# One block for the five stages of a post-norm attention and mixture-of-experts layer

## What is computed

```python
q, k, v = split(x @ Wqkv)            # 16 heads of 16; rotary tables on q and k
attn    = softmax(q @ k.T / 4) @ v   # inside each sequence of 512
x       = layernorm(x + attn @ Wo)
normed  = x * rsqrt(mean(x**2) + 1e-8) * norm_weight
shared  = relu(normed @ sw1 + sb1) @ sw2 + sb2            # 256 -> 1024 -> 256
w, idx  = top2(sigmoid(normed @ router_w.T)), divided by their sum
routed  = sum over the 2 experts e of w_e * (relu(normed @ ew1[e] + eb1[e]) @ ew2[e] + eb2[e])
out     = layernorm(x + shared + routed)                  # 8 experts
```

## Time and profile before

| | us |
|---|---|
| median of 3 runs (lowest, highest) | 1376.45 (1374.98, 1380.32) |
| the profiled execution, its own time | 1369.96 |
| its span, first to last instruction | 1368.1 |
| attention ends (last DVE instruction) | 583 |
| norm_and_route | 586 to 662 |
| shared_and_dispatch | 662 to 799 |
| experts | 804 to 1279 |
| combine | 1286 to 1368 |

### The profile page before, as it was taken

One profiled execution on the slowest core, in us unless ns is written; L12 is line 12 of the kernel. 1 busy time (PEld: TensorE's weight loads), 2 busy tenths in 40 slices (PEclk: granted clock), 3 DMA queues, 4 the chain that ended last, 5 costly groups with the idle time before them and its releaser, 6 DMA issues. The chain is left out here.

```text
span 1368.1 us, 29579 instructions
## 1 busy us (share of the span) xinstructions
PE 1256.6 (92%) x9440; PEld 955.3 (70%) x9440; DVE 1064.5 (78%) x2100; ACT 983.6 (72%) x2010; POOL 598.0 (44%) x550
## 2 busy tenths in 40 slices
PE   3799999999999999869899959999999999999594
PEld 2444444444444444258899959999999999999594
DVE  4688887888788877459576639988988888889498
ACT  5499988999889899748744436666666666666385
POOL 7332322222222210026446725666666666666461
PEclk8799999999999999979899979999999999999897
DMA  9000101010000000352032245666777766665344
GB/s 373 18 17 2 33 2 34 2 33 18 4 18 2 17 2 17 109 170 63 5 113 85 91 142 197 241 228 230 239 242 242 239 228 227 232 230 171 120 143 135
DMA packets 116021, 161.25 MB, mean 118 GB/s; under 512 B 16400, under 2 KB 97552, under 8 KB 114768
## 3 DMA queue, kind: packets, MB, share of 16 engines
q1 hardware_dynamic: 109104, 141.24, 31.1%
q0 software_dynamic: 6816, 18.75, 3.7%
HBM read 122.05 MB, written 37.52 MB: 117 GB/s over the span
## 5 line engine op out<-in xcount | busy, mean ns | idle before, releaser
L495 DVE TENSOR_REDUCE att_mx<-att_psA 128x1 f32<-128x512 f32 x512 | 336.1, 685 | 84.2 <-PE att_psA L297 78.9
L412 ACT ACTIVATE att_prob<-att_psB 128x512 f32<-128x512 f32 x512 | 296.8, 601 | 35.2 <-PE att_psB L307 23.5
L1524 ACT ACTIVATE exp_psU<-exp_psU,ew_b 128x256 f32<-128x256 f32 x312 | 126.6, 444 | 149.9 <-PE exp_psU L1481 149.9
L307 PE MATMUL att_psB<-att_qk 128*128 128x512 bf16 x512 | 196.4, 385 | 12.9 <-DMA att_qk<-att_mrow 9.6
L297 PE MATMUL att_psA<-att_qk 96*128 96x512 bf16 x512 | 196.0, 385 | 2.3 <-DVE att_mx L495 2.3
L1479 PE MATMUL exp_psU<-exp_xh,exp_w1h 128*128 128x256 f32 x624 | 176.7, 283 | 3.1 <-DVE exp_w1l L1553 2.2
L1464 PE MATMUL exp_psD<-exp_w2h,exp_hh 128*128 128x256 f32 x624 | 178.3, 286 | 0.0
L1480 PE MATMUL exp_psU<-exp_xl,exp_w1h 128*128 128x256 f32 x624 | 177.6, 285 | 0.0
L1465 PE MATMUL exp_psD<-exp_w2l,exp_hh 128*128 128x256 f32 x624 | 176.3, 283 | 0.0
L1481 PE MATMUL exp_psU<-exp_xh,exp_w1l 128*128 128x256 f32 x624 | 175.1, 281 | 0.0
L1466 PE MATMUL exp_psD<-exp_w2h,exp_hl 128*128 128x256 f32 x624 | 174.2, 279 | 0.0
(11 more groups left out here) (190 smaller groups left out, 3323.9 us busy)
## 6 DMA issues: line engine op xcount, KB each, us to landing
ew_w<-ew SPq DMA_DIRECT2D x40, 1024.0 KB, 6.6
exp_w<-ew SPq DMA_DIRECT2D x38, 1024.0 KB, 7.1
exp_xs<-slots_x SPq DMA_DIRECT2D x39, 260.0 KB, 4.3
slots_x<-pre_acc SPq DMA_DIRECT2D x9, 1024.0 KB, 15.2
out_g<-rows_y SPq DMA_DIRECT2D x32, 256.0 KB, 3.4
ew_b<-eb SPq DMA_DIRECT2D x39, 128.0 KB, 5.8
att_xt<-xT SPq DMA_DIRECT2D x8, 512.0 KB, 3.7
attn_rows<-att_ob SPq DMA_DIRECT2D x8, 512.0 KB, 3.0
```

What stands on the lines that cost most here:

```text
L307: pe.matmul(psB[B_BANK[n % U]][:, :], r[:, 1, kt * P:(kt + 1) * P], r[:, 0, :], start=True, stop=True).then_inc(s_bmm, 1)
L412: act.activation(prob[:, n % PR, :], psB[B_BANK[n % U]][:, :], ACT.Exp, scale=SCALE).then_inc(s_exp, 1)
L495: dve.reduce_max(mx[:, g % 2, n % U:n % U + 1], psA[A_BANK[n % U]][:, :], AX_X).then_inc(s_max, 1)
```

## The change

The five blocks become one. `Program` holds the one block and `ended`, a list of semaphores with values that tell that the last stage's compute is done; each engine's list for a stage now begins with waits on these (`after_last`) and has no drain or barrier. Semaphores are all held to the end of the kernel. Buffers of a new stage still lie where those of older stages lay.

```diff
+class Program:
+    def __init__(self, nc, ctx):
+        self.block = ctx.enter_context(nc.Block())
+        self.ended = []
+    def after_last(self, eng):
+        for s, v in self.ended:
+            eng.wait_ge(s, v)
...
 # attention, SP, period 29
                     sp.wait_ge(s_const, 2)
+                    sp.wait_ge(s_xl, B)
+                    norm.load_constants(sp, x, Wo, norm_w, router_wT)
                     for b in range(B - 1):
                         ...
                         norm.load_attention(sp, attn_out, b)
...
             for k in range(2):
                 sp.wait_ge(s_ost[k], 16 * (B // 2))
+            norm.load_attention(sp, attn_out, B - 1)
...
 # attention, POOL, two more steps after the eight of the start
+                lambda: pool.memset(norm.eps[:, 0:1], 1e-5),
+                lambda: pool.memset(norm.eps[:, 1:2], 1e-8),
...
+        pr.ended = [(s_onrm, NG)]                               # end of attention
...
 class NormInputs:                         # its spare region is attention's xt buffer
+    def load_constants(self, sp, x, Wo, norm_w, router_wT):
+        x_blk = x.rearrange("(b t p) d -> b p t d", t=self.NT, p=P)
+        sp.dma_start(self.wo, Wo.rearrange("(c p) n -> p c n", p=P)).then_inc(self.s_wo, 16)
+        sp.dma_start(self.first_x, x_blk[0]).then_inc(self.s_xr[0], 16)
+        sp.dma_start(self.rw, router_wT.rearrange("(c p) e -> p c e", p=P)).then_inc(self.s_w, 16)
+        sp.dma_start(self.nw, norm_w.partition_broadcast(P)).then_inc(self.s_w, 16)
...
 # norm_and_route, SP
-            sp.dma_start(wo[:, :, :], Wo.rearrange("(c p) n -> p c n", p=P)).then_inc(s_wo, 16)
-            sp.dma_start(xr[:, 0], x_blk[0]).then_inc(s_xr[0], 16)
-            sp.dma_start(rw[:, :, :], router_wT.rearrange("(c p) e -> p c e", p=P)).then_inc(s_w, 16)
-            sp.dma_start(nw[:, :], norm_w.partition_broadcast(P)).then_inc(s_w, 16)
-            given.load_attention(sp, attn, NB - 1)
+            pr.after_last(sp)
             for b in range(NB):
...
+                if b == 2:
+                    lists.load(sp, tri, marks, homes)           # mk, home, trs of the dispatch
...
 # norm_and_route, POOL: identity and eps are those of attention
-            for k, step in enumerate(( ...memset, affine_select, memset, memset... )):
-                step().then_inc(s_id, 1)
-                pool.wait_ge(s_id, k + 1)
+            pr.after_last(pool)
             pool.wait_ge(s_w, 32)
             pool.wait_ge(s_sw, 64)
...
+        pr.ended = [(s_lcp, TILES), (s_swl, 2 * SWP)]           # end of norm_and_route
...
 # shared_and_dispatch
-            sp.dma_start(mk[:, :], marks).then_inc(s_k, 16)
-            sp.dma_start(home[:, :, :], ...).then_inc(s_home, 16)
-            sp.dma_start(trs[:, :], tri).then_inc(s_k, 16)
+            pr.after_last(sp)
+            weights.load_spare(sp, homes)
...
-            for k in range(2):                                  # POOL
-                pool.wait_ge(s_sc[k], 2 * per_sem)
+        pr.ended = [(shared.added, NB)]
+        return [(s, TILES * 16) for s in s_sc]                  # "sent"
...
 # experts, SP
-            sp.dma_start(spare[:, :, :], homes[...]...).then_inc(s_spare, 16)
+            pr.after_last(sp)
+            for landed in sent:
+                sp.wait_ge(*landed)
...
 # experts, POOL: no identity at the start, no wait at the end
-            pool.memset(ident[:, :], 0.0).then_inc(s_id, 1)
-            pool.affine_select(out=ident[:, :], ...).then_inc(s_id, 1)
+            pr.after_last(pool)
...
-            for k in range(2):
-                pool.wait_ge(s_st[k], 16 * RT * ((NL + 1 - k) // 2))
...
 # experts, ACT (DVE the same with rows_lo and w1_lo)
-            rows_hi(Tile(0))
+            pr.after_last(act)
             for q in range(WP):
                 w1_hi(Tile(0), q)
+            rows_hi(Tile(0))
...
+        pr.ended = [(s_y, NL)]
+        m.landed = [(s_st[k], 16 * RT * ((NL + 1 - k) // 2)) for k in range(2)]
...
 # combine, DVE and ACT
-            dve.memset(eps[:, :], 1e-5).then_inc(s_eps, 1)
+            pr.after_last(dve)
             shared.rows_lo(dve, Nth(0))
...
-            act.wait_ge(s_eps, 1)
...
 # combine, SP
+            pr.after_last(sp)
+            for landed in m.landed:
+                sp.wait_ge(*landed)
```

More of the change, by code:

```diff
@@ L78, in attention @@
         sin = a.sb("sin", [P, NT, DH], F32)
-        xt = a.sb("xt", [P, 2, DC, L], F32)
+        xt = norm.spare[:, :].rearrange("p (k c l) -> p k c l", k=2, c=DC)
         wh = a.sb("wh", [P, DC, 3 * D], F32R)
@@ L654, in norm_and_route @@
         psL = [a.ps(f"psL{i}", [P, 512], F32) for i in range(2)]
-        s_wo, s_w = a.sem("projection_weights"), a.sem("weights")
+        s_wo, s_w, s_xr = given.s_wo, given.s_w, given.s_xr
         s_sw = a.sem("shared_weights")
         s_swh, s_swl = a.sem("shared_hi"), a.sem("shared_lo")
-        s_xr = [a.sem(f"residual_loaded{i}") for i in range(2)]
-        s_id = a.sem("identity")
         s_ttr = a.sem("attn_turned")
@@ L852, in _, with __init__, load @@
                     dve.bn_aggr(mv[:, i % 4, :], st[:, i % 4, :]).then_inc(s_var, 1)
+        pr.ended = [(s_lcp, TILES), (s_swl, 2 * SWP)]
+class DispatchInputs:
+    def __init__(self, pr, ctx, marks, T, D):
+        a = Steps(pr, ctx, "sent")
+        self.trs = a.sb("trs", [P, P], F32)
+        self.mk = a.sb("mk", [P, marks.shape[1]], F32)
+        self.home = a.sb("home", [P, 2, T // P], F32)
+        self.rows = a.sb("rows", [P, T // P, D + HOME], F32)
+        self.s_k = a.sem("constants")
+        self.s_home = a.sem("homes_loaded")
+    def load(self, sp, tri, marks, homes):
+        sp.dma_start(self.mk[:, :], marks).then_inc(self.s_k, 16)
+        sp.dma_start(self.home[:, :, :], homes[:, SPARE // P:].rearrange("p (k t) -> p k t", k=2)).then_inc(self.s_home, 16)
+        sp.dma_start(self.trs[:, :], tri).then_inc(self.s_k, 16)
 class Nth:
@@ L984, in add, with shared_and_dispatch @@
         dve.tensor_tensor(acc, self.psD[n.parity][:, :, :], acc, ALU.add).then_inc(self.added, 1)
[L987 removed]
+def shared_and_dispatch(pr, homes, slots_x, lists, weights, m):
     TILES, E = m.logits.shape[1], m.logits.shape[2]
@@ L1265, in load_first, with experts @@
             load(sp, 0, e)
-def experts(nc, slots_x, weights, homes, rows_y, m):
+def experts(pr, slots_x, weights, sent, ident, rows_y, m):
     w1, w2, b1, b2 = weights.w1, weights.w2, weights.b1, weights.b2
@@ L1291, in experts @@
         xs = a.sb("xs", [P, 2, RT, slots_x.shape[1]], F32)
-        home = a.sb("home", [P, 4, RT], U32)
-        spare = a.sb("spare", [P, 2, RT], F32)
+        w1h = a.sb("w1h", [P, DC, HID], F32R)
+        w1l = a.sb("w1l", [P, DC, HID], F32R)
+        spare, s_spare = weights.spare, weights.s_spare
         xh = a.sb("xh", [P, 2, DC, LT], F32R)
@@ L1775, in layer @@
     with ExitStack() as ctx:
-        given = NormInputs(nc, ctx, T, P * rope_cos.shape[1], D)
-        attention(nc, xT, Wqkv, rope_cos, rope_sin, attn, slots_x, given)
-        m = Carried(nc, ctx, given.acc, T, D, E, sw1.shape[1], LT)
-        weights = ExpertWeights(nc, ctx, ew1, eb1c, ew2, eb2)
-        with nc.sbuf_tensor("all_rows", [P, T // P, D + HOME], F32) as rows:
-            norm_and_route(nc, x, attn, Wo, norm_w, router_wT, sw1, sb1c, sw2, sb2, rows, given, m)
-            shared_and_dispatch(nc, tri, marks, homes, slots_x, rows, weights, m)
-        experts(nc, slots_x, weights, homes, rows_y, m)
-        combine(nc, rows_y, out, m)
+        pr = Program(nc, ctx)
+        given = NormInputs(pr, ctx, T, P * rope_cos.shape[1], D, E)
+        attention(pr, x, xT, Wqkv, rope_cos, rope_sin, Wo, norm_w, router_wT, attn, slots_x, given)
+        m = Carried(pr, ctx, given.acc, T, D, E, sw1.shape[1], LT)
+        with ExitStack() as until_used:
+            weights = ExpertWeights(pr, until_used, ew1, eb1c, ew2, eb2, LT)
+            with ExitStack() as until_sent:
+                lists = DispatchInputs(pr, until_sent, marks, T, D)
+                norm_and_route(pr, x, attn, sw1, sb1c, sw2, sb2, tri, marks, homes, lists, given, m)
+                sent = shared_and_dispatch(pr, homes, slots_x, lists, weights, m)
+            experts(pr, slots_x, weights, sent, given.ident, rows_y, m)
+        combine(pr, rows_y, given.eps, out, m)
 def kernel(L0_attn_x, L0_attn_Wqkv, L0_attn_Wo, L0_ffn_norm_weight, L0_ffn_router_w, L0_ffn_sw1, L0_ffn_sb1,
```

135 lines of the change are left out of this document (68 added, 67 removed).

## The result

The median went from 1376.47 us (1374.98 to 1380.32) to 1356.01 us (1353.51 to 1356.50), four runs each: ratio 0.984, 95% interval 0.983 to 0.986. The forecast was 1360.0 us, range 1354 to 1367.

The account below looks back on a forecast made before the run. The prediction looked to the four unequal seams between stages, not their arithmetic. Its terms, 7.0 + 6.7 + 0.2 + 5.5 - 3.0 = 16.4 us, took the median from 1376.45 to 1360.0 us, eight in ten from 1354 to 1367.

Parts of the forecast that it names:

- the norm stage's rate changed: Norm stage: the forecast counted itself wrong if this stage's rate, rather than its start, had changed.
- attention ended later than 588: End of attention: 586 us was expected in place of 583; later than 588 would show the forecast wrong.
- (a): Experts to combine: SP waits for landings alone, so combine's loads go out earlier; gain 7.0 us, bounds 6.1 and 10.5.
- Rival 2: Both scatter seams: idle time is no drain but paid by others too; total gain 4.7 us, 1371.7 us; chance 0.08.
- (b): Shared to experts: list 0's load goes out earlier and weights are split before the rows; gain 6.7 us, bounds 5.7 and 7.3.
- (c): Norm to shared: the 0.28 us barrier goes and waits remain; gain 0.2 us, bounds 0 and 0.9.
- (d): Attention to norm: the last bias lands earlier, so POOL's first multiplication starts earlier; gain 5.5 us, bounds 3.5 and 6.5.
- Rival 3: Norm stage: ACT or DVE late, or bias issued late, so (d) gains only 3 us; 1362.5 us; chance 0.15.
- (e): End of attention: constants queued ahead of the last group's maxima make PE wait longer; loss 3.0 us, bounds 0 and 5.
- rival 1: Last group of attention: the maxima are not held up by the constants; gain 19.4 us, 1357.0 us; chance 0.22.
- Inside the stages the change alters no arithmetic: Whole kernel: the prediction's premise, so it looked for gains only in what lies between the stages, at four seams.

Follow-up runs that it names:

- set 2: Four kernels on one chip beside the kernel before (1372.97 us): the kernel before again, its reordered buffers, the changed kernel with barriers at quiet seams, and the changed kernel again.
- late_constants: Changed kernel with the four constants issued where they were before, behind the landing of attention's last sequence: 1395.18 us, ratio 0.991 to the kernel before.
- blocks_at_quiet_seams: Changed kernel with a new block (drain and barrier) put back at attention to norm and norm to shared: 1356.09 us, ratio 0.988 to the kernel before.
- before_new_order: Kernel before with only the experts' SBUF buffers allocated in the changed kernel's order: 1366.94 us, ratio 0.996 to the kernel before.
- before_again: The kernel before, unchanged, profiled once more on the chip of set 2: 1371.34 us.
- after_third: The changed kernel, unchanged, run again on the chip of set 2: 1353.65 us, ratio 0.987 to the kernel before.
- split_later: early_again, with POOL's first multiplication not waiting for the shared expert's weights and their splitting 6 tiles later: 1388.19 us, ratio 0.981 to the kernel before.
- sets 1 and 2: Two sets of follow-up runs, each on its own chip; the unchanged changed kernel was rerun in both: 1390.52 us (0.987) and 1353.65 us (0.987).
- early_again: Changed kernel with the four constants issued in period 25 in place of 29, repeated on another chip: 1395.65 us, ratio 0.986 to the kernel before.
- sets 1 and 3: Two sets of follow-up runs, each on its own chip, beside the kernel before at 1409.21 us and 1414.0 us.

## Why the prediction was right, and where its terms were off

The time fell inside the range and on the forecast's side. Two of the signs that the prediction had named against itself did appear: the norm stage's rate changed, beside its start, and attention ended later than 588 (at 594.54; with the start and the loop of the kernel before it would be 588.3). Both are taken up below. By its steps:

- **(a) Experts to combine, 7.0.** Measured 6.7 (11.45 to 4.70; also 6.7 in set 2). That it is the block's end and not a landing that others pay too is shown: a block put back there costs 5.26 us twice (2.45 to 7.71). Rival 2 fell. The other 1.5 us go with POOL's wait for the landing in front of that end (9.2 against 7.71). The early start of the other engines brought nothing: from the first load on the stage took 1.1 us longer (0.2 in set 2).
- **(b) Shared to experts, 6.7.** Last scatter to first product 15.04 to 8.05 us, 7.0. Of this 6.1 is the seam and 0.9 the earlier split of the weights. The prediction called the moved `spare` load off this path; it was on it, with 0.4 of the 6.1 us. Same mechanism as (a), but shown here only between whole kernels.
- **(c) Norm to shared, 0.2.** The last logits end at 669.47, ACT's first instruction of the next stage starts at 669.50, in place of 0.28 us behind the earlier trace rows.
- **(d) Attention to norm, 5.5.** Measured 6.2, in set 2 5.2; 15.3 us was forecast for the gate and 14.6 to 15.4 came. late_constants gives 5.6 us to the loads' place, blocks_at_quiet_seams some 0.4 to the barrier. Rival 3 fell.
- **(e) The maxima held up, 3.0.** This is the term that was mis-sized: 5.3 us (5.5 in set 2). The wait was seen almost right (4.80 us, "about 4" forecast), and rival 1 fell with it. What was missing is that PE comes out of such a pause at half clock: 3.8 us more wait and 1.5 us for the restart at 0.50. I had bounded it at 5, by the loads alone. The maxima, issued at 570.13, released PE only at 577.30, behind a burst that ended at about 575. (The rows that the prediction cites for the queue's order are of ten transfers, not nine.) The Trainium skill, page "DMA: Bandwidth & Descriptors", section "Queues, rings and completion order", says that a DMA engine takes the descriptors of one issuer's ring in ring order; the trace agrees in that the maxima did not get past the burst (4.1 to 5.2 us to landing in place of 1.7), while two of them landed before the last load that was issued ahead of them.

Together 6.7 + 7.0 + 0.3 + 6.2 - 5.3 = 14.9 us, 1.5 less than summed. The medians differ by 20.5. The other 5.5 us are sought in stretches where I took the change for nothing:

- The experts' pace, -5.7 us (470.53 to 463.85 less the 0.9 of (b)). "Inside the stages the change alters no arithmetic" was true and not enough: it moves buffers. before_new_order shows 26 of 42 products in 400 us from addresses alone.
- The norm stage's rate, +2.0 us in the first profile and +1.3 in set 2. Its last 12 us, before_again first, then after_third (granted clock is the third number from the end):

```profile
657.70:663.70 6.00, 4.37 (x31) 3.58 (x29) 5.39 (x25) 5.04 (x21) 2.87 (x5) 1.00 0.00 0
663.70:669.70 6.00, 4.07 (x25) 3.72 (x25) 0.84 (x2) 4.31 (x14) 0.29 (x1) 0.66 0.04 10
```

```profile
655.90:661.90 6.00, 4.36 (x29) 3.64 (x29) 5.58 (x25) 5.03 (x21) 2.87 (x5) 0.94 0.00 0
661.90:667.90 6.00, 5.41 (x28) 5.31 (x26) 0.16 (x1) 3.92 (x14) 0.54 (x1) 0.50 0.00 0
```

 With nearly as many products in the last 6 us (25 and 28), PE needs 5.41 us in place of 4.07: in the tail, where it is partly idle, the clock falls to half (1.2 GHz) some 2.5 us sooner, counted from POOL's first multiplication (both pairs of rows begin 48 us after it). Why sooner was not found; it does so with barriers at the quiet seams too (59.64 us). That is the 1.3 us of set 2. Of the 2.0 us of the first profile the greater part, 1.2 us, arises at the stage's start: POOL's seventh multiplication comes 12.80 us behind its first in place of 11.55 (603.82 to 615.37 before, 609.15 to 621.95 after), and the granted clock of these first 12 us is 0.72 in place of 0.81.
- The rest is scatter between executions: the loop differs by up to 7 us between executions of either kernel (503.8, 505.9 and 509.6 us in the three profiles of before and its variant, 506.5 to 511.0 in the eleven of after and its variants). It took 7.2 us more in the first profile after, and with as long a loop as before the two profiled executions would be 21 us apart. Whether the change has a small part in it is open: the three have a mean of 506.5, the eleven of 509.1, on different chips.

So the forecast was right for four of its five steps. That it came within 4 us is in part luck: a cost that was put too small (e) and a gain that it did not have (the pace) went against each other.

**A better version.** split_later has the lowest ratio of all, 0.981 (0.978 to 0.984), against 0.984 (0.983 to 0.986) for the changed kernel in the first comparison and 0.987 in sets 1 and 2. It was run on one chip only, and not beside the changed kernel; beside early_again it is 0.5% faster with intervals that overlap a little, and its landmarks (7.1 us) say the same.

## What to carry to other kernels

Look at what POOL had in flight when a block ends: behind arithmetic a barrier here costs some 0.3 to 0.4 us, right behind an indirect DMA 5 us and more, and a wait on the landing's semaphore replaces it. A load that is "moved to where there is time" goes into a queue: name what stands behind it, and move it past the last small transfer that PE waits for (here four periods earlier saved 5.5 us there and cost at most 0.7 at the gate). And before taking a gate at a seam as a queue's fault, ask whether the waiting instruction needs what it waits for: in split_later 7 us came from taking out one such wait, with the splits of the weights moved later to allow it.

## What the hardware showed that I had not expected

- SBUF addresses change the pace of a stage that PE bounds, without idle time and at full clock: 11.805 us a list against 11.716 by the order of the buffers alone. The changed kernel, whose buffers lie differently again and which has other differences too, takes 11.657.
- On two of the chips PE lost 30 to 50 us in the shared stage while the indirect scatters ran. Stretches of 25 us, after_third (set 2) and then early_again (set 3):

```profile
725.00:750.00 25.00, 25.00 (x213) 25.00 (x212) 15.76 (x38) 11.98 (x30) 17.63 (x18) 1.00 0.25 91
```

```profile
721.00:746.00 25.00, 13.28 (x59) 10.81 (x58) 5.65 (x12) 3.62 (x8) 17.56 (x19) 0.66 0.27 96
...
796.00:821.00 25.00, 24.93 (x195) 24.55 (x195) 15.57 (x37) 11.91 (x29) 0.00 (x0) 0.93 0.00 0
```

 The scatters keep their rate (19 against 18 instructions on POOL, 96 against 91 GB/s), but PE does 59 products in place of 213. Its waits in early_again, 696 to 786:

```profile
ACT shr_h L991 <- remote: 31.7, 7, 19.3
...
DVE shr_hl L1006 <- issue: 21.4, 5, 17.0
```

 DVE once stood 17 us with nothing in the profile to wait for, and ACT waited up to 19.3 us for a releaser that the profile can't name ("remote"). As soon as the scatters end, PE is full again (195 products). All eight profiles of sets 1 and 3 end their shared stage that late, and the kernel before is 33 to 41 us over its time on the other chips there, so it seems not to be the change's; no profile of the kernel before was taken on these chips. The cause is open. A late supply of instructions would fit the engines' idle time, but the table of DMA queues speaks against the plainest form of it: from 725 to 850 in early_again no packet is recorded on either of the two queues that the profile labels "instruction" (nor from 725 to 796 in after_third), and the scatters' queue moved 6.39 MB in both. On such a chip the seam from shared to experts hides nothing and gains nothing, since the scatters aren't last.
